# Output projection of 31 of 32 quads as seven block products in place of eight

## The reference

```python
kv_c = kv @ W_kvc                       # 512 x 256
q_c = q @ W_dq                          # 512 x 384
q_nope = (q_c @ W_uq) per head (16 x 128);  q_rope = rope(q_c @ W_qr) per head (16 x 64)
k_nope = (kv_c @ W_uk) per head;  v = (kv_c @ W_uv) per head;  k_rope = rope(kv_c @ W_kr), one for all heads
scores = (q_nope . k_nope + q_rope . k_rope) / sqrt(192)
good = (k_ids <= seg_id) & (k_ids >= seg_id - 8);  attn = softmax(where(good, scores, -1e30))
out = (attn @ v).reshape(b, lq, H * HD)
x = x + out @ W_o                       # W_o: 2048 x 1024
```

## Time and profile before

| | |
|---|---|
| median of 3 runs | 3063.37 us (3063.0 to 3065.53) |
| profiled execution, span (no other time is recorded for it) | 3064.5 us |
| PE busy | 2988.8 us, 98% |
| DVE / ACT / POOL busy | 68% / 50% / 23% |
| granted clock of PE, in tenths | 9 in each of 40 slices |
| DMA | 162 GB/s mean, 47.9% of the 16 engines' span in the hardware queue |

### The profile page before, as it was taken

The page is one execution under the profiler, slowest core; times in us unless marked ns, Lnnn a source line. Parts: engine busy times, 40 slices in busy tenths (PEclk is TensorE's granted clock), DMA queues, the critical chain, the costliest instruction groups (busy, mean ns, idle before and its releaser), DMA issues.

```text
span 3064.5 us, 40912 instructions
## 1 busy us (share of the span) xinstructions
PE 2988.8 (98%) x14258; PEld 2436.3 (79%) x14258; DVE 2086.9 (68%) x4515; ACT 1528.7 (50%) x2990; POOL 701.8 (23%) x528
## 2 busy tenths in 40 slices
PE   8999999999999999999999999999999999999985
PEld 6788878888888888888888888888888888888862
DVE  4555657777577767777577775777757776667777
ACT  3656535554455544555354552655535554555553
POOL 6222141111411123111411114111141112311127
PEclk9999999999999999999999999999999999999985
DMA  7654465444644446444563446544364444634431
GB/s 251 241 177 156 171 224 179 146 146 151 225 144 141 135 161 233 138 130 146 198 212 128 128 134 214 202 136 147 127 247 145 132 147 171 210 127 145 143 93 4
DMA packets 164553, 496.74 MB, mean 162 GB/s; under 512 B 36848, under 2 KB 50800, under 8 KB 139648
## 3 DMA queue, kind: packets, MB, share of 16 engines
q1 hardware_dynamic: 159280, 493.26, 47.9%
q0 software_dynamic: 5072, 0.88, 0.6%
HBM read 387.94 MB, written 72.55 MB: 150 GB/s over the span
## 4 chain that ended last, share of the span: by engine, by line
PE 93%; DVE 3%; ACT 1%; issue 1%; POOL 1%; DMA 1%; SPq 0%; ACTq 0%; POOLq 0%; DVEq 0%
PE psC L2240 11%; PE psD L2231 10%; PE psE L2240 10%; PE psA L2156 9%; PE psT L2218 7%; PE psB L2165 6%; PE psD L2176 4%; PE psS L2192 4%; PE psS L2193 4%; PE psS L2205 4%; PE psS L2201 4%; PE psS L2202 4%; PE psA L2108 3%; PE psA L2147 2%; PE psB L2147 2%; PE psB L2108 2%
## 5 line engine op out<-in xcount | busy, mean ns | idle before, releaser
L1194 ACT ACTIVATE exps_ring<-exps_ring,neg_max 128x512 f32<-128x512 f32 x512 | 370.9, 724 | 404.9 <-DVE neg_max L1565 404.1
L1565 DVE CUSTOM_DVE_ANT_0 exps_ring<-psS,mask 128x512 f32<-128x512 f32 x512 | 353.2, 690 | 287.5 <-PE psS L2205 282.1
L1208 ACT ACTIVATE probsT_hi<-psT 128x512 fp32r<-128x512 f32 x472 | 282.2, 598 | 342.1 <-PE psT L2218 338.7
L1200 ACT ACTIVATE exps_ring<-exps_ring,row_sum_inverse 128x512 f32<-128x512 f32 x512 | 369.7, 722 | 60.9 <-DVE row_sum_inverse L1571 60.9
L1577 DVE TENSOR_TENSOR probsT_lo<-psT,probsT_hi 128x512 fp32r<-128x512 f32 x472 | 324.0, 686 | 58.2 <-ACT probsT_hi L1208 57.2
L2240 PE MATMUL psC<-w_o_pair,attn_hi 128*128 128x512 f32 x1016 | 333.3, 409 | 0.7 <-DVE attn_lo L1583 0.7
L2240 PE MATMUL psE<-w_o_pair,attn_hi 128*128 128x512 f32 x896 | 295.3, 410 | 0.0
L2218 PEld LDWEIGHTS psT<-ident,exps_ring 128*128 128x128 f32 x1888 | 228.4, 140 | 76.1 <-issue 25.5
L2218 PE MATMUL psT<-ident,exps_ring 128*128 128x128 f32 x1888 | 283.2, 272 | 4.5 <-DVE probsT_lo L1577 3.6
L2156 PE MATMUL psA<-q_c_hi,w_uq_ring 128*128 128x512 f32 x768 | 260.6, 393 | 0.1
L2192 PE MATMUL psS<-k_hi,q_hi 128*128 128x512 f32 x512 | 202.3, 395 | 0.8 <-ACT k_rope_hi L1183 0.8
(11 more groups left out here) (440 smaller groups left out, 6411.8 us busy)
## 6 DMA issues: line engine op xcount, KB each, us to landing
w_o_pair<-w_o_split SPq DMA_DIRECT2D x112, 1024.0 KB, 5.6
w_uq_ring<-w_uq_split SPq DMA_DIRECT2D x114, 384.0 KB, 4.0
w_uv_quad<-w_uv_split SPq DMA_DIRECT2D x29, 1024.0 KB, 4.9
w_uk_ring<-w_uk_split SPq DMA_DIRECT2D x114, 256.0 KB, 2.8
w_qr_sorted<-w_qr_split SPq DMA_DIRECT2D x29, 768.0 KB, 4.2
x_stage<-in_x_dram SPq DMA_DIRECT2D x32, 512.0 KB, 6.3
x_stage<-in_ctx_dram SPq DMA_DIRECT2D x32, 512.0 KB, 4.5
q_rope_stack<-rope_hi SPq DMA_DIRECT2D x256, 64.0 KB, 3.4
```

Of the source, the lines that this page charges most:

```text
L1194: act.activation(E[:, qt, :], E[:, qt, :], ACT.Exp, scale=-1.0, bias=mx[:, i % 2, qt:qt + 1], accum_out=rs[:, i % 2, qt:qt + 1]).then_inc( ...
L1200: act.activation(E[:, qt, :], E[:, qt, :], ACT.Copy, scale=ri[:, i % 2, qt:qt + 1]).then_inc(s_prob, 1)
L1565: dve.tensor_tensor_reduce(E[:, qt, :], psS[qt % 2][:, :], mask[:, qt, :], -SCALE, BIG, ALU.add, ALU.min, mx[:, i % 2, qt:qt + 1]).then_in ...
```

## The change

The output projection of a quad (512 tokens x 512 K by 1024 columns) is cut into 2x2 blocks: token tiles of even and odd number, head pairs, column halves. Of eight block products seven are made (products 0 to 6), from sums and differences of blocks. A product is two groups `u` of six matmuls, so a quad has 14 groups in place of 16. Only the last quad of the last batch keeps the old form. Part by part:

- TensorE: `product` replaces `out_proj` and `out_end`; products 2, 3 and 4 are accumulated onto what their bank holds.
- Order: `groups` says which group stands in which step. A quad's products now begin in head 0 of the next quad (steps 0 and 1), then one group a step in heads 1 to 3; quad 0 of a batch has none. The last of quad 2 and all 14 of quad 3 stand in the batch's border.
- Attention: ACT copies psD into `attn` in f32 (L1471), and POOL makes four sums a quad (`sum_of_quad`, `late_sums`). Each product gets its own split operand: `product_hi` (ACT, 7 a quad) and `product_lo` (DVE, 7 a quad, both inputs in SBUF), in a ring of two. The subtraction `attended_lo` (4 a quad) goes. `attended` now waits for sums and low parts of the quad before.
- Adds: 12 plain and 2 of double width a quad on DVE, in place of 16.
- Weights: `w_o_split` holds one entry of 1 MB for each product of a quad, 28 loads a batch in place of 16, each into slot n % 2 when product n-2 is done.
- Batch 0: the sums and differences of the raw weights are made on POOL (`wo_sum`, 5 a quad), and seven split entries a quad in place of four.
- Some buffers are laid over others to make room.

The core of the diff:

```diff
-    def pos_o(b, q, pair, w):
-        n = 2 * q + pair
-        return b * EN + n * 4 + q + pair + w // 2 if w % 2 else b * CN + TT // 2 + n * 4 + w // 2
+        def groups(b, q, i, step):
+            if q == 0:
+                return []
+            if i == 0:
+                return [(q - 1, 0, step)] if step < 2 else []
+            if i == HQ - 1 and q == NQ - 1 and b < B - 1:
+                return [[(q - 1, 5, 0)], [(q - 1, 5, 1)], [], [(q - 1, 6, 0)]][step]
+            return [(q - 1, 2 * i - 1 + step // 2, step % 2)]
...
-            def load_o(b, q, pair, half):
-                n = q * 2 + pair
-                if q == 0 and pair == 0:
-                    sp.wait_ge(fullC, b * CN)
-                    sp.wait_ge(fullD, b * DN)
-                else:
-                    sp.wait_ge(fullE, pos_o(b, (n - 1) // 2, (n - 1) % 2, 3 + 4 * half) + 1)
+            def load_o(b, q, j):
+                n = prod_no(b, q, j)
+                product_done(sp, n - 2)
+                sp.dma_start(WO[:, n % 2].rearrange("p s i n -> p (s i n)").bitcast(F32),
+                             flat(wo_dram[bass.ds(q, 1), j])).then_inc(s_wo[n % 2], 16)
...
                 load_uk(b, q, 2, (q, 0))
                 if q > 0:
-                    load_o(b, q - 1, 1, 0)
+                    load_o(b, q - 1, 0)
                 stack_head(b, q, HQ - 1)
+                if q > 0:
+                    load_o(b, q - 1, 1)
...
+            def sum_of_quad(b, q, k):
+                base = (b * NQ + q) * SUM_ALL
+                if base + k > 0:
+                    pool.wait_ge(s_asum, base + k)
+                if k == 0:
+                    pool.wait_ge(freeD, pos_av(b, q, 1) + 1)
+                    if b + q > 0:
+                        pool.wait_ge(s_aplo, prod_no(b, q, 4) - NP + 1)
+                    pool.tensor_tensor(asum4, quarter(0, 0), quarter(0, 1), ALU.subtract).then_inc(s_asum, 1)
+                elif k == 1:
+                    pool.wait_ge(freeD, pos_av(b, q, HQ - 1) + 1)
+                    pool.tensor_tensor(quarter(0, 1), quarter(0, 1), quarter(1, 1), ALU.add).then_inc(s_asum, 1)
...
+            def attended(b, q, i):
+                act.wait_ge(fullD, pos_av(b, q, i) + 1)
+                if b + q > 0:
+                    act.wait_ge(s_asum, (b * NQ + q) * SUM_ALL)
+                    act.wait_ge(s_aplo, prod_no(b, q, 3 if i < 2 else 6) - NP + 1)
...
+            def product_lo(b, q, j):
+                n = prod_no(b, q, j)
+                dve.wait_ge(s_aphi, n + 1)
+                dve.tensor_tensor(operand_part(n, 1), operand(j), operand_part(n, 0).bitcast(F32), ALU.subtract)\
+                   .then_inc(s_aplo, 1)
+            def add_product(b, q, j, u):
...
+                if j == 0:
+                    a = acc[:, t + 1, :].rearrange("p (a n) -> p a n", a=2)
+                    twice = ps[:, :].rearrange("p (a n) -> p a n", a=1).broadcast_to([P, 2, HALF])
+                    dve.tensor_tensor(a, a, twice, ALU.add).then_inc(free, 1)
+                    return
...
+            def product(b, q, j, u):
+                n = prod_no(b, q, j)
+                if u == 0:
+                    pe.wait_ge(s_wo[n % 2], 16 * (n // 2 + 1))
+                    pe.wait_ge(s_aplo, n + 1)
+                ps, full, free = product_bank(q, j, u)
+                wait_free(free, pos_p(b, q, j, u))
+                if q + j == 0 and u == 1:
+                    pe.wait_ge(s_ptlo, tile_no(b, 0, 2, 1) + 1)
+                goes_on = j in (2, 3, 4)
+                for i in range(2):
+                    for a, o in ((0, 0), (0, 1), (1, 0)):
+                        mm_ = pe.matmul(ps[:, :], operand_part(n, a)[:, i, u, :], WO[:, n % 2, o, i, :],
+                                        start=i + a + o == 0 and not goes_on, stop=i + a == 2, skip_group_check=goes_on)
+                mm_.then_inc(full, 1)
...
+                turn_probs(b, o, HQ - 1, 2)
+                turn_stage(b + 1, 0, False)
+                product(b, o - 1, 6, 1)
+                turn_probs(b, o, HQ - 1, 3)
+                product(b, o, 0, 0)
+                turn_stage(b + 1, 1, False)
+                product(b, o, 0, 1)
+                attend(b, o, HQ - 1)
+                turn_stage(b + 1, 2, False)
+                product(b, o, 1, 0)
+                product(b, o, 1, 1)
+                turn_stage(b + 1, 3, False)
+                product(b, o, 2, 0)
+                product(b, o, 2, 1)
+                down_q(b + 1)
```

More of the change, by code:

```diff
@@ L479, in load_xs @@
                 elif b == 1:
-                    for half in range(2):
-                        sp.wait_ge(s_wo[half], 16 * (PAIRS - 2))
+                    for n in (2 * NP - 2, 2 * NP - 1):
+                        sp.wait_ge(s_wo[n % 2], 16 * (n // 2 + 1))
                 elif not (b == 0):
@@ L900, in uq_lo, with late_sums @@
+            def late_sums(b, q):
+                for k in range(1, SUM_ALL):
+                    sum_of_quad(b, q, k)
             def uq_lo(q, i, raw):
@@ L1237, in prologue, with sums_hi @@
                         uk_hi(0, i, 1, uk_raw0)
-                for j in range(2, TT):
-                    stage_turned(b, j, False)
+                def sums_hi(*js):
+                    for j in js:
+                        if not first:
+                            product_hi(b - 1, NQ - 1, j)
+                        if b == 1 and j >= 5:
+                            wo_hi(NQ - 1, j)
+                stage_turned(b, 2, False)
+                sums_hi(2, 3)
+                stage_turned(b, TT - 1, False)
+                sums_hi(4)
+                if b == 1:
+                    wo_hi(NQ - 1, 3)
+                    wo_hi(NQ - 1, 4)
                 if first:
@@ L1305, in head @@
                         turned(b, q, i, 0)
+                    if q > 0 and i == 2:
+                        product_hi(b, q - 1, 5)
+                    if i == HQ - 1 and not plain_quad(b, q):
+                        product_hi(b, q, 0)
+                    if first and q > 0 and i < 2:
+                        wo_hi(q - 1, (1, 3)[i])
                     if head0:
@@ L1807, in head @@
                     piece(2)
-                    if not head0 and not late:
+                    if q > 0 and i == 1:
+                        product_lo(b, q - 1, 3)
+                    if i > 0 and plain_quad(b, q):
                         attended_lo(b, *before)
@@ L1826, in head @@
                     invert(b, q, i, 3)
-                    if late:
-                        attended_lo(b, *before)
                     if i == 0 and not q0:
                         values_lo(b, q, 0)
-                    add_last()
+                    if q > 0 and i == 2:
+                        product_lo(b, q - 1, 5)
+                    if i == HQ - 1 and not plain_quad(b, q):
+                        product_lo(b, q, 0)
+                    add(3)
                     piece(3)
@@ L2426, in body @@
-                for t in range(TT):
-                    if last:
-                        continue
-                    if t < TT - 2:
-                        out_end(b, t, 0)
-                        out_end(b, t, 1)
-                    elif t == TT - 2:
-                        out_end(b, t, 0)
-                    if not last and t == 1:
-                        turn_stage(b + 1, 3, False)
-                if not last:
-                    down_q(b + 1)
-                    turn_stage(b + 1, 0, True)
-                    turn_stage(b + 1, 1, True)
@@ L2539, in out_last @@
                     split = pos_av(B - 1, NQ - 1, HQ - 1) + 1 if t == 0 and half == 0 else None
-                    project(ps, 1, half, t, split).then_inc(full, 1)
+                    project(ps, (wl2, WO[:, ring_last % 2])[half], 1, t, split).then_inc(full, 1)
             out_last(0)
```

646 lines of the change are left out of this document (436 added, 210 removed).

## The result

The changed kernel takes 3340.14 us (median of 4 runs, 3334.9 to 3344.15), the kernel before 3064.21 in the same comparison: ratio 1.0899, 95% interval 1.0884 to 1.0915. It is 276 us slower, where 201 were forecast. The profiled execution has a span of 3336.0 us, 271.5 more than before.

A forecast was written before the change was run, and what follows sets the result against it. TensorE, busy for 98% (2988.8 of 3064.5 us), was taken as the bound, with no slack to hide waits. Batches 1 to 6 +152, last batch +22, batch 0 +27 make +201: 3264 us, range 3155 to 3340.

The forecast's parts named there:

- the rival of crowded transfers: 28 loads in place of 16 land near 9.2 us, 3 us more in 21 places: 3345 us, chance 0.12.
- The load in front of the last head's rope parts comes late for step 0: Head 0, quads 1 to 3: product 0's weights, queued behind rope DMAs, land 5.5, 5.4 and 5.2 us late.
- The gain of quad 0 falls into the same hole: Quad 0's five removed groups save nothing: product 0 of quad 1 still starts 5.5 us later than before.
- The clock behind product 0's waits: After each long wait TensorE runs 3.40 us at half clock, losing 1.7 us; three waits a batch, 5.1.
- The rival without it: Waits as forecast but the clock kept: 3226 us, or 3186 or 3154 with smaller waits; chance 0.35.
- The gain: 62 output groups fewer on TensorE at 1.42 us each: 88 us saved in all.
- The rate of 0.131 us a matmul: The skill's sustained-stream rate, set beside the forecast's own: 372 matmuls worth 49 us, not 88.
- The small waits: Short TensorE waits in the heads: 0.8 us in quads 1 and 2, 1.4 in quad 3.
- The turning bank: Some 0.5 us of wait where no group stands between turnings: step 3 of head 0, again in quad 3's head 3.
- The border: Border to the next batch: four groups more, +5.7 us, and waits of 5.3, together +11.0.
- Batch 0: Heads -14.1 us, weight waits +13.5; border +15 for POOL's weight work, +11 as elsewhere, clock 2: together +27.
- 0.3 us an operation: VectorE's 217 new low parts slowed beside POOL: 65 us at most, a twentieth, 3 us, counted.

The follow-up runs named there:

- e2: Kernel before, with only an added TensorE wait in step 0 of head 0 for the load until then needed in step 3: 3220.68 us, ratio 1.0507.
- e1: Changed kernel with the load of product 0's weights moved ahead of the sixteen rope DMAs in the SP queue: 3166.67 us, ratio 1.0325.
- e5: Kernel of e4 with three changes of order (second groups of products 0 and 5, POOL's border sums, DVE's low part of product 2): 3118.92 us, ratio 1.0174.
- e7: Kernel before with 288 matmuls of its output projection left out and nothing else altered: 3007.36 us, ratio 0.9812.
- e4: Kernel of e1 with product 0's double-width adds and the last x tile's load moved earlier in the border: 3135.87 us, ratio 1.0232.
- e6: Kernel of e5 with batch 0's sums and differences of output weights computed for only 8 of 512 columns: 3103.3 us, ratio 1.0126.
- e8: Kernel of e6 with batch 0's low-part subtraction of output weights also cut to 8 of 512 columns from the third product on: 3080.28 us, ratio 1.0047.

## Why the prediction was right, and where it was off

The mechanism and its place were right. The time lay 76 us above the forecast, on the very edge of the range (3340), and that it did not fall out of it is luck. It also lies near the price of the rival of crowded transfers, 3345 (its terms add up to 3347), but not by that rival's mechanism: loads of 1 MB landed after 5.8 us in the median, for 5.6 before.

```profile
DMA to landing us min/median/max: 4.6/5.8/12.6
```

Step by step:

- *The load in front of the last head's rope parts comes late for step 0.* Right, in size as well: 9.75 us of issues were read from the earlier trace rows, and the changed trace has 9.72. In quads 2 and 3 the waits were 5.1 and 5.3 us on average, for 5.4 and 5.2, and their loads landed after 6.3; the 7.3 shown above is one of the slower ones. In quad 1 the wait was 7.9, but TensorE reached it 2.9 us sooner, so product 0 started 4.9 later than before, for 5.5. e2, which takes no group out, has 5.24 a wait. e1 and e2 show the wait from both sides.
- *The gain of quad 0 falls into the same hole.* Right for what there was of it: quad 0's head 3 is 2.9 us shorter, and head 0 of quad 1 is 8.5 us longer, against 5.6 in quads 2 and 3. But five groups are worth 6 us. The other 3 went before the hole: with these groups gone, TensorE waits, nearly always in quad 0, for the query and rope parts that VectorE makes: 25.1 us in the two lines `q_lo` and the line `rope_term` above, where the kernel before has one such wait of 0.9. The forecast had no such term, and in e5, where the weights are in time, quad 0 is still only 2.9 us shorter.
- *The clock behind product 0's waits.* Forecast 1.7 us a wait from one row of idle time, 5.1 a batch. Measured 2.0 in e2 (42.7 / 21) and 2.1 between the changed kernel and e1 (3014.7 - 2969.7 of busy time, for 21). Right, mis-sized by a fifth. The rival without it is refuted.
- *The gain.* 1.42 us a group was too much. In e5, where no wait is left in head 0 of quads 2 and 3, two groups fewer make it 2.5 us shorter, 1.26 each; e7 gives 1.19 for six matmuls. Against 88, the 62 groups are worth 74 to 78. The term was mis-sized by 10 to 14 us. The rate of 0.131 us a matmul, which the forecast had set beside its own from the Trainium skill, "TensorE: Matmul & The Clock Gate", section "Back-to-back issue gap", is further off: e7 would have come to 3026.
- *The small waits.* The turning bank was read right in kind, and counted too low in number: 34.5 us in 76 waits, which is 9 to 10 a batch where I had 4. One of them, 0.43 us, stands in each head 1, for which the forecast had 0.3 of another kind.
- *The border.* Forecast +11.0, of which 5.3 are waits. The +14.2 measured are counted from the start of head 3, which has a group fewer and a small wait more; for that stretch the forecast comes to +10.1. TensorE was idle for 7.1 to 7.9 us where it was for 0.85 to 1.1, +6.4 for 5.8: product 2's operand 1.8 us (forecast 2), the adds in front of the down projection 2.0 (forecast 3.3), and, missed, the last x tile 1.6, whose load now stands behind 1 MB of weights and whose normalisation runs beside POOL's sums (below). Its busy time grew by 7.8. In e4's borders at clock 1.00 the same work adds 4.8, for 4.3 forecast. The remaining 3.0 are clock, a term that the forecast had at nothing there.
- *Batch 0.* This is the term that failed: +53.6 for +27, over a third of the whole error. The failed step is the clock in it, put at 2 us without a working. From the windows above: idle time grew by 40.8 us, where the forecast had 36.7 (2.9 of small waits and 13.5 for weights, 15 and 5.3 for the border); but busy time grew by 12.8 with eight groups fewer, which are worth 8 to 10 (8 less busy time in e5's batches 1 to 6 at clock 1.00, 10 by 1.26 a group). So by this estimate 21 to 23 us are clock, 0.95 and 0.90 for 0.99 and 0.98 before. The heads alone came to +22.3, where the forecast's terms for them add up to nothing. Nor is the idle time all of the kind forecast: the waits for POOL's weights are 17.5 us for 28.5, and others were not foreseen, for rope parts (5.8), the weights of the down projection (5.1 and 3.3) and the x tile (5.1 for 2.4). e6 and e8 show that POOL's work on the weights is behind 36 us of the whole.

Summed by e2 and the stages: of the 276 us, 127 are the waits for product 0's weights and 45 the clock behind them (e1: 173 together); 31 more go with the order of the border (e4), 17 with that of e5, 39 with POOL's work on weights in batch 0 (e6, e8). What is left in e8 is 15 us over the kernel before, a kernel with 372 matmuls fewer and a part of its work left out. Its trace says where the gain went: TensorE is busy for 2929.8 us, 59 less than before, and idle for 152 in place of 76. The waits that remain, many and short, outweigh the matmuls saved. No order of this scheme that was tried beats the kernel before. What stays open is whether batch 0 in the old form and the seven products from batch 1 on would; in e5 batches 1 to 6 are within 2.6 us of before each and batch 7 is 3.9 shorter, which together is 0.5 us of gain, so it could not gain much.

## What to carry to other kernels

Where one engine is busy for 98%, work taken out of it is only worth something if every new dependency is ready when it asks: look up in the order of the DMA queue what stands in front of each load that is now needed earlier. Here the sixteen issues ahead of it (0.6 us each) took longer than its own landing. Add to each wait of 4 to 9 us on TensorE some 2 us for the clock that follows it, and look for the clock in every stage that gets new waits. Ask too what the matmuls that go were covering: in quad 0 half of what they gave back went to waits for VectorE. A scheme that saves an eighth of one phase and adds sums, operands and loads to four other engines has to win back more than it saves.

## What the hardware showed that was not expected

A VectorE operation with its operands in SBUF that starts while a POOL `TENSOR_TENSOR` runs ends only after that one has ended, 0.54 us behind it or more. In the border of batch 3 of the changed kernel (POOL's sums and the normalisation of the x tile):

```profile
1624.56 1.27 POOL L1103 TENSOR_TENSOR attn<-attn 128x512 f32<-128x512 f32 x1
1624.63 1.75 DVE L1765 TENSOR_SCALAR x_stage<-x_stage,ln_mean_var 128x1024 f32<-128x1024 f32 x1
...
1625.90 1.61 POOL L1106 TENSOR_TENSOR attn<-attn 128x512 f32<-128x512 f32 x1
```

and in that of batch 0:

```profile
414.59 2.34 POOL L1084 TENSOR_TENSOR w_o_product<-w_o_room_of_last_quad,w_o_product 128x1024 fp32r<-128x1024 f32 x1
414.73 2.75 DVE L1765 TENSOR_SCALAR x_stage<-x_stage,ln_mean_var 128x1024 f32<-128x1024 f32 x1
416.88 2.81 POOL L1074 TENSOR_TENSOR w_o_room_of_last_quad<-w_o_room_of_last_quad 128x1024 f32<-128x1024 f32 x1
...
417.53 1.97 PE L2415 MATMUL psS<-ident,x_stage 128*128 128x128 f32 x8 [5.06 <-DVE x_stage L1765]
```

The normalisation takes 0.80 us with POOL idle, 1.75 beside a sum of 1.27 and 2.75 beside a subtraction of 2.34: in both it ends 0.55 us after the POOL operation. The POOL operation behind it is longer too, 1.61 us where the one before took 1.27 for the same shape, and 2.81 where such sums take some 2.4. TensorE waited for 5.06 us for that second one, of which the stretch is 1.95. The prediction had put this at 0.3 us an operation from the earlier trace rows.

It is so in every case of the changed trace. All 21 normalisations that start inside a `TENSOR_TENSOR` of POOL end 0.54 to 0.55 us after it. Of the 217 low parts, 157 ran free of POOL, 0.676 us on average; 38 started inside such an operation, took 1.02 on average and up to 2.53, and none ended sooner than 0.54 us after it. Two things bound it. Twelve low parts that started inside a `TENSOR_SCALAR` of POOL took 0.68 to 0.71, though up to 1.35 us of that operation were still to run (the addition of the earlier trace rows, beside such an operation, did take 1.00). And eight low parts of the kernel before, which read PSUM, started inside a `TENSOR_TENSOR` and took 0.692, the same as the free ones.

The Trainium skill, "GPSIMD Engine Reference", section "1. Specifications", names contention with VectorE instructions that have two SBUF inputs or run in a 2-port perf mode. The low parts have two SBUF inputs and agree. The normalisation has one input tensor; whether it runs in such a mode no view here names, but it does 1024 columns in 0.80 us where a low part needs 0.68 for 512.

The same 1 MB load takes 4.6 to 12.6 us to land in the changed kernel; only the longest got longer, the median is 5.8 for 5.6.
